# Attention on one core: energies from fp32 queries and keys on four blocks of 32 rows, in bursts of four, in place of split bf16 pieces

## The reference

```python
C4 = C // 4
xc = jnp.transpose(x, (0, 2, 1))
q = jnp.einsum('oc,bcn->bno', Wq, xc)
k = jnp.einsum('oc,bcn->bon', Wk, xc)
energy = jnp.einsum('bno,bom->bnm', q, k)
attn = jax.nn.softmax(energy, axis=-1)
attn = attn / (1e-06 + jnp.sum(attn, axis=1, keepdims=True))
x_r = jnp.einsum('bcn,bnm->bcm', xc, attn)
d = xc - x_r
t = jnp.einsum('oc,bcn->bon', Wt, d) + bt[None, :, None]
bn = gamma[None, :, None] * (t - bn_mean[None, :, None]) * jax.lax.rsqrt(bn_var[None, :, None] + BN_EPS) + beta[None, :, None]
out = xc + jnp.maximum(bn, 0.0)
```

## Time and profile before

| | us |
|---|---|
| median of three runs (3213.0 to 3220.93) | 3215.72 |
| the profiled execution | 3216.21 |
| its span in the profile | 3214.5 |
| first to last energy (line 1805) | 1667.3 to 2608.5 |
| TensorE busy over the span | 2288.7 (71%) |
| VectorE busy | 2227.2 (69%) |
| ScalarE busy | 1623.1 (50%) |

### The profile page before, as it was taken

One profiled execution on the slowest core, in us unless ns is written; L12 is line 12 of the kernel. 1 busy time (PEld: TensorE's weight loads), 2 busy tenths in 40 slices (PEclk: granted clock), 3 DMA queues, 4 the chain that ended last, 5 costly groups with the idle time before them and its releaser, 6 DMA issues. The chain is left out here.

```text
span 3214.5 us, 46923 instructions
## 1 busy us (share of the span) xinstructions
PE 2288.7 (71%) x15979; PEld 1511.7 (47%) x15979; DVE 2227.2 (69%) x4935; ACT 1623.1 (50%) x3184; POOL 1042.7 (32%) x1059
## 2 busy tenths in 40 slices
PE   5999804655756656527749999999999994403996
PEld 3555403555655555414415455455445553401775
DVE  2888846889899898439957768767777755400776
ACT  1444326667676676224456755664764631101664
POOL 0455501222122222139912222222122222273555
PEclk9999956877778778667769999999999995556998
DMA  6477748657657453462230002001001003012221
GB/s 180 100 182 162 179 115 220 172 148 197 174 144 186 139 147 88 107 258 80 79 82 1 1 1 60 1 1 37 24 1 31 11 10 104 5 41 90 90 90 52
DMA packets 343238, 304.60 MB, mean 95 GB/s; under 512 B 73775, under 2 KB 299703, under 8 KB 341536
## 3 DMA queue, kind: packets, MB, share of 16 engines
q1 hardware_dynamic: 334208, 294.00, 33.3%
q0 software_dynamic: 8800, 7.70, 0.8%
HBM read 158.50 MB, written 156.80 MB: 98 GB/s over the span
## 5 line engine op out<-in xcount | busy, mean ns | idle before, releaser
L1913 ACT ACTIVATE attn_prob<-attn_ps_e,attn_nm 128x448 f32<-128x448 f32 (+1 forms) x700 | 438.7, 632 | 324.5 <-DVE attn_nm L2000 321.9
L1817 PE MATMUL attn_ps_r<-attn_prob,attn_xs 128*128 128x448 f32 (+1 forms) x1400 | 585.7, 548 | 5.0 <-POOL attn_xs L1719 5.0
L940 PE MATMUL deform_ps_w<-all_ident,deform_grid 128*126 128x128 f32 x1568 | 268.0, 337 | 316.3 <-DVE deform_grid L1025 199.9
L2000 DVE TENSOR_REDUCE attn_nm<-attn_ps_e 128x1 f32<-128x448 f32 (+1 forms) x700 | 407.7, 615 | 36.7 <-PE attn_ps_e L1805 34.7
L866 POOL MEMSET deform_grid<- 128x3752 f32 (+1 forms) x64 | 187.1, 2924 | 709.1 <-PE deform_ps_w L940 663.4
L1716 POOL TENSOR_TENSOR attn_xs<-attn_xa,attn_wz 128x381 f32<-128x381 f32 (+1 forms) x200 | 184.4, 946 | 715.8 <-DVE attn_wz L2021 715.8
L940 PEld LDWEIGHTS deform_ps_w<-all_ident,deform_grid 128*126 128x126 f32 x1568 | 231.6, 176 | 351.5 <-DVE deform_grid L1025 211.3
L1817 PEld LDWEIGHTS attn_ps_r<-attn_prob,attn_xs 128*128 128x128 f32 (+1 forms) x1400 | 263.5, 192 | 208.2 <-issue 176.8
L900 ACT ACTIVATE deform_wt<-deform_ps_w 126x896 f32<-126x896 f32 x224 | 203.5, 933 | 227.5 <-PE deform_ps_w L940 143.1
L885 ACT ACTIVATE deform_hat<-deform_rel,block_negr 128x504 f32<-128x504 f32 (+1 forms) x256 | 258.6, 1124 | 104.0 <-DVE deform_rel L985 103.7
L1025 DVE TENSOR_TENSOR deform_grid<-deform_grid,deform_prod 128x448 f32 (+1 forms) x512 | 297.8, 582 | 8.8 <-DVE deform_grid L1025 7.9
(11 more groups left out here) (321 smaller groups left out, 4131.1 us busy)
## 6 DMA issues: line engine op xcount, KB each, us to landing
deform_xw<-shifted SPq DMA_DIRECT2D x112, 504.0 KB
shifted<-deform_xm SPq DMA_DIRECT2D x8, 4032.0 KB, 12.4
offsets_masks<-offs_om SPq DMA_DIRECT2D x48, 378.0 KB
deform_om<-offsets_masks SPq DMA_DIRECT2D x48, 378.0 KB
dispatched<-rows_zero SPq DMA_DIRECT2D x1, 16512.0 KB, 48.7
experts_bi<-dispatched SPq DMA_DIRECT2D x32, 516.0 KB, 3.5
deform_xa<-projected SPq DMA_DIRECT2D x64, 168.0 KB
projected<-offs_zero SPq DMA_DIRECT2D x13, 680.0 KB
```

The lines of the kernel that those rows point to most:

```text
L940: mm = pe.transpose(ps_w[n % 2][0:NPOS, q * LANES:(q + 1) * LANES], grid[:, u % 2, at:at + NPOS], ident[:, :])
L1817: mm = pe.matmul(ps_r[n % 2][:, 0:BK], xs[0:rows, at + i, j, :], prob[0:rows, at + i, j * BK:(j + 1) * BK], start=(i == 0), stop=(i == len ...
L1913: nc.scalar.activation(prob[0:rows, slab(S) + i, ch * BK:(ch + 1) * BK], ps_e[u % NE][0:rows, 0:BK], ACT.Exp, bias=nm[0:rows, S % 2, i, ch ...
L2000: nc.vector.tensor_reduce(nm[0:rows, S % 2, i, ch:ch + 1], ps_e[u % NE][0:rows, 0:BK], AX, ALU.max, negate=True).then_inc(mx_ok, 1)
```

## The change

Queries and keys stay fp32. One copy each (`query_kept`, `keys_kept`) takes all four row blocks, which hold the same 32 channels, out of PSUM into `qf` and `kf`. Unit u's energies are one fp32 matmul over the 32 rows of block u % 4. In TensorE's order the energies of four units u, u+1, u+2, u+3 (u a multiple of 4) all get the number u, so they stand together; sums, queries and the rest keep their numbers. All piece steps and their buffers and semaphores go, and with them the zeroing at the start. The number of banks stays five. VectorE's and ScalarE's orders lose the piece steps and are otherwise the same.

```diff
+NROW = 4
...
     for u in range(B * UNITS):
-        pe.append((u, "energy", u))
+        pe.append((u // NROW * NROW, "energy", u))
         dve.append((u + 0.1, "max", u))
         act.append((u + 0.2, "exp", u))
...
         pe.append((at + 0.7, "query", S))
-        act.append((at + 0.8, "query_hi", S))
-        dve.append((at + 1.15, "query_rest", S))
-        act.append((at + 1.3, "query_mid", S))
-        dve.append((at + 3.15, "query_low", S))
+        act.append((at + 0.8, "query_kept", S))
...
-            act.append((at + lag + 0.8, "keys_hi", n))
-            dve.append((at + lag + 1.15, "keys_rest", n))
-            act.append((at + lag + 1.3, "keys_mid", n))
-            dve.append((at + lag + 1.4, "keys_mid_too", n))
-            dve.append((at + lag + 3.15, "keys_low", n))
+            act.append((at + lag + 0.8, "keys_kept", n))
...
-        released = {"turn": xT_ok, "keys": k_ok, "query": q_left, "columns": c_ok, "own": sx_ok, "others": un_ok}
+        released = {"turn": xT_ok, "keys": k_ok, "query": q_ok, "columns": c_ok, "own": sx_ok, "others": un_ok}
...
                     if u >= NE:
                         pe.wait_ge(ex_ok, u - NE + 1)
                     rows, at = tile_rows(tile), i * 128
-                    for q_, k_ in ((qa, ka), (qb, kb)):
-                        mm = pe.matmul(ps_e[u % NE][0:rows, 0:BK], q_[:, S % 2, at:at + rows],
-                                       k_[:, b % 2, ch * BK:(ch + 1) * BK], start=q_ is qa, stop=q_ is qb)
-                    mm.then_inc(e_ps, 1)
+                    own = slice(u % NROW * C4, (u % NROW + 1) * C4)
+                    pe.matmul(ps_e[u % NE][0:rows, 0:BK], qf[own, S % 2, at:at + rows], kf[own, b % 2, ch * BK:(ch + 1) * BK],
+                              start=True, stop=True).then_inc(e_ps, 1)
...
+                def keys_kept(n):
+                    b, g = divmod(n, NG)
+                    cols = group_cols(g)
                     act.wait_ge(k_ps, n + 1)
-                    nc.scalar.activation(kb[C4:2 * C4, b % 2, cols], bank("keys", n)[C4:2 * C4, 0:w], ACT.Copy)
-                    nc.scalar.activation(ka[:, b % 2, cols], bank("keys", n)[:, 0:w], ACT.Copy).then_inc(k_hi, 1)
+                    nc.scalar.activation(kf[:, b % 2, cols], bank("keys", n)[:, 0:cols.stop - cols.start], ACT.Copy)\
+                        .then_inc(k_ok, 1)
...
+                def query_kept(S):
                     w = query_width(S)
                     act.wait_ge(q_ps, S + 1)
-                    nc.scalar.activation(qb[0:C4, S % 2, 0:w], ps_x[0:C4, 0:w], ACT.Copy)
-                    nc.scalar.activation(qa[:, S % 2, 0:w], ps_x[:, 0:w], ACT.Copy).then_inc(q_hi, 1)
+                    nc.scalar.activation(qf[:, S % 2, 0:w], ps_x[:, 0:w], ACT.Copy).then_inc(q_ok, 1)
```

More of the change, by code:

```diff
@@ L1611, in attention_stage @@
         ps_x = t.ps("ps_x", [128, 512])
[L1612 to L1613 removed]
+        (w_in, wT, w_ok, bstep, bn_done, const_ok, xT, xT_ok, k_ps, k_ok, q_ps, q_ok, e_ps, mx_ok, ex_ok, sstep, dm_ok, ez_ok, w_rdy, xs_ok, r_ps, r_ok, c_ps, c_ok, rc_ok,
          ux_ps, sx_ok, ur_ps, un_ok, tin_ok, t_ok) = [
              t.sem(s) for s in (
[L1616 to L1618 removed]
+                 "weights_loaded weights_turned weights_ready bn_step bn_done constants_ready xT_in_psum xT_ready "
+                 "keys_in_psum keys_ready query_in_psum query_ready energy_in_psum max_ready exp_ready soft_step below_ready "
                  "rescale_ready chunk_weights_ready xs_ready sums_in_psum sums_added columns_in_psum columns_read "
@@ L1794, in energy @@
                     if ch == 0 and i == 0:
-                        pe.wait_ge(qs_ok, S + 1)
+                        pe.wait_ge(q_ok, S + 1)
                         if S % NSB == 0:
[L1797 to L1800, removed]
+                            pe.wait_ge(k_ok, (b + 1) * NG)
                     if u >= NE:
@@ L1928, in _ @@
                         turned(i)
-                    elif step == "keys_hi":
-                        keys_hi(i)
-                    elif step == "keys_mid":
-                        keys_mid(i)
-                    elif step == "query_hi":
-                        query_hi(i)
+                    elif step == "keys_kept":
+                        keys_kept(i)
                     else:
-                        query_mid(i)
+                        query_kept(i)
             @block.vector
             def _(dve):
-                for i in range(2):
-                    nc.vector.memset(kb[2 * C4:4 * C4, i, :], 0.0).then_inc(zeroed, 1)
-                    nc.vector.memset(qb[2 * C4:4 * C4, i, :], 0.0).then_inc(zeroed, 1)
                 dve.wait_ge(bstep, 2)
@@ L1955, in _ @@
                 dve.wait_ge(w_ok, 1)
-                def keys_rest(n):
-                    b, g = divmod(n, NG)
-                    cols = group_cols(g)
-                    w = cols.stop - cols.start
-                    dve.wait_ge(k_hi, n + 1)
-                    if n >= 2:
-                        dve.wait_ge(k_step, n - 1)
-                    nc.vector.tensor_tensor(k_rest[:, n % 2, 0:w], bank("keys", n)[:, 0:w], ka[:, b % 2, cols],
-                                            ALU.subtract).then_inc(k_ok, 1)
-                def keys_mid_too(n):
-                    cols = group_cols(n % NG)
-                    w = cols.stop - cols.start
-                    dve.wait_ge(k_ok, n + 1)
-                    nc.vector.tensor_copy(k_mid[:, n % 2, 0:w], k_rest[0:C4, n % 2, 0:w]).then_inc(k_more, 1)
-                def keys_low(n):
-                    b, g = divmod(n, NG)
-                    cols = group_cols(g)
-                    w = cols.stop - cols.start
-                    dve.wait_ge(k_more, n + 1)
-                    nc.vector.tensor_tensor(kb[0:C4, b % 2, cols], k_rest[0:C4, n % 2, 0:w], k_mid[:, n % 2, 0:w],
-                                            ALU.subtract).then_inc(k_low, 1)
-                def query_rest(S):
-                    w = query_width(S)
-                    dve.wait_ge(q_hi, S + 1)
-                    if S:
-                        dve.wait_ge(q_step, S)
-                    nc.vector.tensor_tensor(q_rest[:, 0:w], ps_x[:, 0:w], qa[:, S % 2, 0:w], ALU.subtract)\
-                        .then_inc(q_left, 1)
-                def query_low(S):
-                    w = query_width(S)
-                    lo = slice(C4, 2 * C4)
-                    dve.wait_ge(q_step, S + 1)
-                    nc.vector.tensor_tensor(qb[lo, S % 2, 0:w], q_rest[lo, 0:w], q_mid[lo, 0:w], ALU.subtract)\
-                        .then_inc(qs_ok, 1)
                 def row_max(u):
```

35 lines of the change are left out of this document (1 added, 34 removed).

## The result

The changed kernel takes 3254.86 us (median of 4 runs, 3252.50 to 3256.81) against 3214.36 for the kernel before (4 runs, 3212.90 to 3220.93): a ratio of 1.0122, 95% interval 1.0104 to 1.0139, so it is slower by 1.2%, 40 us. The profiled execution took 3252.5 us, span 3250.8.

A forecast was written before the change was run, and what follows sets the result against it. TensorE, busy 910.1 of 943.0 us, was taken to bound the attention stage. The terms 85 + 6 + 19 - 27 - 11 - 4 = +68 on 3216.2 us gave 3284 us, range 3185 to 3385.

The forecast's parts named there:

- light stretches: Attention while a two-tile slab is summed: 13.1 us per 12 units for 10.56 before, +85 us over 19 stretches.
- heavy ones: Attention while a three-tile slab is summed: 6.07 to 6.11 us per burst for 6.02 before, +6 us over 20 stretches.
- The chain: Attention: last energy, sum, add, maxima up to the third, its exponential, next burst's last energy; +85 us where two-tile slabs are summed.
- Slab ends: Small softmax steps on VectorE, a little over 1 us, join the wait at one end per slab pair: +19 us.
- Slack used: Other TensorE work in attention, 83 us beside two-tile sums, hides in TensorE's new idle time by a third: -27 us.
- Four at once: Four fp32 energies on row blocks up to the sum: 1.44 us, bounds 1.08 to 1.83, for 1.52 before.
- No pieces at the start: Ahead of the first energy, one copy each of keys and query: -11 us (-9, to -17 if the clock rises).
- The clock: TensorE's granted clock in attention: below 0.9 would be a cost not in the sum; no size given.
- no difference: Rival for the whole kernel: only a third of the 110 us of waits and slab ends shows, 3211 us; chance 0.08.
- TensorE stays the bound: Rival in attention: four energies at 1.08 against 1.52 take 77 us off, 15 for pieces, 3124 us; chance 0.13.
- Staircase: Rival in attention: each energy's second record holds up the next energy, 2.2 us for four, 3360 us; chance 0.14.
- no overlap: Rival in attention: four energies run one after another in 3.0 us, 3500 us; chance 0.10.

The follow-up runs named there:

- the waits filled: Changed kernel with TensorE repeating the third energy of a burst twice in the 32 bursts that waited over 0.5 us for the last energy's bank: 3216.81 us.
- late adds: Changed kernel with VectorE's adds of all slabs placed behind the four maxima of a burst instead of between them: 3152.60 us.

## Why the prediction was right, and where it was not

The sign was right and the time lies in its range, 29 us under the forecast. The sum that led there had one term missing and others mis-sized, which partly cancel; that the sign came out is in part luck, as the clock below shows. Of the 36.3 us between the two profiled spans: light stretches +35.7 and heavy ones -7.2, both with the waits filled, so with most of the clock's fall taken out; +30.3 that the clock adds to these (507.0 - 489.8 and 478.4 - 465.3); -19.2 at the start; the stage itself began 1.6 earlier; -1.7 elsewhere.

*The chain* was there, link by link, and the order was its cause: bursts alone slow the bf16 kernel, and moving the adds removes the loss. Its size: a cycle at the full clock took 12.89. Per 21 units that is 22.6 for 18.5, 19 times +78, where I had 85.

*Slab ends* did not add their 19. In four light slabs, two in the first batch and two in the last, hardly anything but a query stands beside the energies and sums; with the waits filled they grew, slab end included, by 2.6, 4.0, 4.0 and 2.1 us (from 21.13, 21.14, 21.14 and 21.03). That is 3.2 on average, or 60 us for 19 slabs, less than the cycle alone gives and far from my 85 + 19.

*Slack used* was about right: all light stretches together grew by 36, so by this measure some 24 of the 83 us of other work hid in the waits. I had taken a third, 27. The split is an estimate: by the cycle's 78 it would be 42.

*Four at once* was mis-sized most. I took 1.44, between 1.08 and 1.83; it is 0.96 (1757.51 to 1758.47), under my lower bound: next to a lone energy's 0.94 to 0.95 the three neighbours add nothing, loads included. I had read the column blocks' 31 ns as loads in turn, and carried that to row blocks, which don't show it. The way back from a sum to row blocks is 0.20, not 0.12. So a heavy burst in which no energy waits takes 5.67 for 6.02 before, where I had 6.07 to 6.11; in every burst that would be 3.5 x 20 x 0.35 = 24 us of gain. With the waits filled 7 are left. Some 7 went to the lower level (41 us at 0.54 for 27); the other 10 are a remainder, and waits inside bursts, as at 1763.18, and bursts of two widths (last section) are a part of it. The Trainium skill ("TensorE: Matmul & The Clock Gate", Measured speedup vs the span model) gives 3.07 for four row tiles; the trace agrees: four times two records of 0.376 are 3.0, and 0.96 is 3.1 times less.

*No pieces at the start* gave 19.2, not 11. The upper end, 17 if the clock rises, was the nearer: the clock rose (granted 0.99 from 1638.0 to 1646.5, for 0.51 from 1649.0 to 1660.0 before), and keys went 1.30 us apart, not 2.6. The -4 for later pieces lies in stretches that other terms moved, and no run shows it by itself.

*The clock* was no term of the sum. I named it only as a cost outside the sum, below 0.9; the stage is at 0.93, and that already costs 30 us, up to 38 by the medians. Without it, in the kernel with the waits filled, the time is 3217 us, which is the rival "no difference" (3211) and not my forecast. So the sign hangs on a loss I had not foreseen, although one that the chain's waits bring about: with the waits filled, or the adds late, it goes.

*What would show it:* VectorE's wait for sums grew as said. TensorE's idle time was to rise above 100 us; it is 35.8, since the waits lie inside the records of bursts. That test was badly chosen: the row to ask is the weight loads' wait for exponentials, 127.5 us for 46.5 before.

*The rivals:* "TensorE stays the bound" has come true in the version with late adds, where the chain is mostly gone and four cost 0.96: 3153 us, for the 3124 I had given. Staircase and no overlap are out: two, three and four energies take the same 0.95 to 0.96 up to the next sum.

## What to carry to other kernels

Where a burst uses nearly all buffers of a ring, a step that its consumer does between two of its items can become a wait for the producer, if that step itself waits for work behind the burst; move such steps behind the burst before judging the burst. Here two changes that were each worth nothing or a loss (fp32 row blocks with the old order of adds, the new order with bf16) made 2% together. And where short waits of TensorE appear, read the granted clock of those stretches before and after: the long waits were 40 us, and the clock that fell behind them cost 30 more, at instructions that had not changed.

## What the runs showed of the hardware

- On row blocks, fp32 energies of 32 x 448 take the same time up to the next sum whether one (0.94 to 0.95 us), two (0.95), three (0.95 to 0.96) or four (0.96) go together; at the lower clock four take 1.80.
- They go together only if they are of one width. In the six bursts where energies of a tile of 64 queries meet those of a tile of 128, the two kinds follow one another, and the next instruction starts after 1.85 us (2.00 in one), for 0.91 in a burst of 64 alone; with late adds, so without the chain's waits, it is 1.85 in all six. One of them in the changed kernel, with three energies of 64 and one of 128:

```profile
1859.95 1.92 PE L1791 MATMUL attn_ps_e<-attn_kf,attn_qf 32*64 32x448 f32 x8
1861.80 2.52 PE L1802 MATMUL attn_ps_r<-attn_prob,attn_xs 128*128 128x448 f32 x6
```

- A kernel was faster by 38 us with 64 matmuls more in it, since TensorE did not idle: granted clock 0.97 for 0.93.
- In these runs the fall needs both: with bf16 energies in bursts, waits of 0.9 us and more leave the clock at 0.98, and the fp32 energies with fewer or shorter waits (78 us by the weight loads with late adds, 104 with bursts of three, for 127.5) leave it at 0.97. Why only the two together bring it to 0.93 stays open.
